# Joining two sequences' causal attentions into one call of eight head groups

## The reference

```
q = (x @ Wq).reshape(b, t, 16, 8) * 8 ** (-0.25)
k = (x @ Wk).reshape(b, t, 16, 8) * 8 ** (-0.25)
v = (x @ Wv).reshape(b, t, 16, 8)
dot = einsum('bqhd,bkhd->bhqk', q, k)
dot = where(causal, dot, -inf)
out = einsum('bhqk,bkhd->bqhd', softmax(dot), v).reshape(b, t, 128)
return out @ Wo
```

## Time and profile before

| | us |
|---|---|
| median of three runs (4137.76 to 4142.01) | 4139.68 |
| the profiled execution | 4147.65 |
| its span, first to last instruction | 4145.7 |
| PE busy in the span | 3816.1 (92%) |
| DVE, ACT, POOL busy | 2304.2, 1747.5, 813.5 |
| mean granted clock of PE | 0.98 |

### The profile page before, as it was taken

One profiled execution on the slowest core, in us unless ns is written; L12 is line 12 of the kernel. 1 busy time (PEld: TensorE's weight loads), 2 busy tenths in 40 slices (PEclk: granted clock), 3 DMA queues, 4 the chain that ended last, 5 costly groups with the idle time before them and its releaser, 6 DMA issues.

```text
span 4145.7 us, 77057 instructions
## 1 busy us (share of the span) xinstructions
PE 3816.1 (92%) x30311; PEld 2466.6 (59%) x30431; DVE 2304.2 (56%) x7434; ACT 1747.5 (42%) x3560; POOL 813.5 (20%) x1373
## 2 busy tenths in 40 slices
PE   7999999988899999998899989999889998999988
PEld 3555567665455556766545546676654555666665
DVE  4545444677454545467654554546765454454776
ACT  3324333466332433346633242335663334233566
POOL 3102013321110202332011020233302102023330
PEclk9999999999999999999999999999999999999999
DMA  2000000000000000000000000000000000000000
GB/s 81 1 1 1 1 1 1 2 2 1 12 1 1 1 1 1 1 2 2 5 8 1 1 1 1 1 1 2 2 6 7 1 1 1 1 1 1 2 2 6
DMA packets 19694, 17.06 MB, mean 4 GB/s; under 512 B 2604, under 2 KB 18941, under 8 KB 19325
## 3 DMA queue, kind: packets, MB, share of 16 engines
q1 hardware_dynamic: 19325, 11.99, 1.0%
HBM read 9.89 MB, written 2.10 MB: 3 GB/s over the span
## 4 chain that ended last, share of the span: by engine, by line
PE 70%; DVE 11%; ACT 8%; POOL 7%; issue 4%; DVEq 0%; POOLq 0%; SPq 0%
PE banks L1033 8%; PE banks L1047 8%; PE banks L1043 8%; PE banks L926 6%; PE banks L958 5%; POOL work L507 4%; PE banks L970 3%; PE banks L911 3%; PE banks L1142 3%; PE banks L1277 2%; ACT work L783 2%; PE banks L831 2%; ACT work L777 2%; PE banks L1114 2%; PE banks L1087 2%
## 5 line engine op out<-in xcount | busy, mean ns | idle before, releaser
L1454 DVE CUSTOM_DVE_ANT_0 work<-banks,mask_row 128x512 f32<-128x512 f32 (+3 forms) x1024 | 444.2, 487 | 248.3 <-PE banks L926 246.3
L669 ACT ACTIVATE work<-banks 128x384 f32<-128x384 f32 (+1 forms) x768 | 357.6, 532 | 373.9 <-PE banks L958 372.2
L687 ACT ACTIVATE work<-banks 128x512 f32<-128x512 f32 (+1 forms) x384 | 227.7, 596 | 650.7 <-PE banks L1043 641.8
L926 PE MATMUL banks<-work 32*128 32x512 f32 (+3 forms) x2048 | 421.5, 460 | 13.0 <-ACT work L662 13.0
L958 PE MATMUL banks<-work 32*128 32x512 f32 (+3 forms) x2048 | 425.8, 464 | 4.3 <-DVE work L1463 4.3
L474 POOL TENSOR_SCALAR_AFFINE_SELECT work<-work 128x128 f32<-128x128 f32 (+1 forms) x768 | 250.1, 332 | 878.8 <-ACT work L669 860.5
L1531 DVE TENSOR_TENSOR work<-work,banks 128x512 f32<-128x512 f32 (+1 forms) x384 | 261.1, 686 | 280.2 <-PE banks L1047 280.2
L464 POOL TENSOR_TENSOR rstd<-rstd,half 128x4 f32<-128x4 f32 x64 | 64.6, 1009 | 1755.2 <-DVE rstd L1388 1755.2
L1033 PEld LDWEIGHTS banks<-wd,work 128*128 128x128 f32 (+1 forms) x3072 | 359.3, 191 | 49.1 <-issue 49.1
L1033 PE MATMUL banks<-wd,work 128*128 128x128 f32 (+1 forms) x3072 | 361.1, 274 | 0.0
L926 PEld LDWEIGHTS banks<-work 32*128 32x128 f32 x2048 | 232.4, 183 | 167.1 <-DVE work L1454 93.6
(11 more groups left out here) (312 smaller groups left out, 6723.0 us busy)
## 6 DMA issues: line engine op xcount, KB each, us to landing
wg<-in_L_ffn_Wg_dram SPq DMA_DIRECT2D x1, 1376.0 KB
wu<-in_L_ffn_Wu_dram SPq DMA_DIRECT2D x1, 1376.0 KB
x_a<-in_L_attn_a_x_dram SPq DMA_DIRECT2D x4, 256.0 KB, 2.8
x_b<-in_L_attn_a_x_dram SPq DMA_DIRECT2D x4, 256.0 KB, 2.9
wd<-in_L_ffn_Wd_dram SPq DMA_DIRECT2D x2, 512.0 KB
out_dram<-x_a SPq DMA_DIRECT2D x4, 256.0 KB, 2.3
out_dram<-x_b SPq DMA_DIRECT2D x4, 256.0 KB, 2.5
wk_l<-in_L_attn_a_Wk_dram SPq DMA_DIRECT2D x1, 512.0 KB, 6.2
```

The lines of the kernel that those rows point to most:

```text
L669: eng.activation(prob4[:, G % 2, hh, C_AT[j]:C_AT[j] + C_N[j]], bank(column_bank(c))[:, 0:C_N[j]], ACT.Exp).then_inc(s_exp, 1)
L926: m = eng.matmul(bank(k % 3)[:, col:col + N], q4[own, G, P * t:P * t + P], k4[own, G, 0:N], start=True, stop=True)
L1454: m = eng.tensor_tensor_reduce(out=summed[:, k % 2, col:col + N], in0=bank(k % 3)[:, col:col + N], in1=mask_row[:, T - N:T], scale=1.0, sc ...
```

## The change

The attentions of a and b of one layer become one call `attn(p)` with eight groups: g = 0 to 3 are a's, g = 4 to 7 b's. Row and column jobs run through 96 steps with the same distance of 16 between them. What b's call did ahead of its jobs, and what a's did behind them, is put behind single row jobs by a table, `BEHIND`: the norm of b behind row job 27, its eight projections behind 39, 42, 51, 54, 63, 65, 77 and 80, its values behind 67, the transposes of a's output behind 75 and its projection behind 79. These entries go round the same three banks as the row jobs (`PLACES`, `row_bank`), and each waits for the entry three places before it. ACT copies an entry's bank behind exponential k - 18. DVE makes the statistics of b's norm behind row maximum 20 and its rows behind 24; POOL makes the power behind select 2. The tail of a and the head of b fall away.

```diff
+GROUPS = 2 * NG
+JOBS = ROWS4 * GROUPS
 LEAD = 16
-WIDE = JOBS4 - LEAD + 1
-HOOK = JOBS4 - 6
+WIDE = JOBS - LEAD + 1
+HOOK = JOBS - 6
+
+
+BEHIND = {27: ("norm", 0), 39: ("project", 8), 42: ("project", 9), 51: ("project", 10), 54: ("project", 11),
+          63: ("project", 12), 65: ("project", 13), 67: ("values", 0), 75: ("out_columns", 0),
+          77: ("project", 14), 79: ("out", 0), 80: ("project", 15)}
+PLACES = [entry for k in range(JOBS) for entry in [("row", k)] + ([BEHIND[k]] if k in BEHIND else [])]
+PLACE = {entry: at for at, entry in enumerate(PLACES)}
...
+        def row_bank(entry):
+            return PLACE[entry] % 3
...
+        def pool_attn(eng, p):
+            for c in range(JOBS):
+                g, hh, j = c // ROWS4, column_head(c), c % ROWS4 // G4
+                eng.wait_ge(s_exp, JOBS * p + c + 1)
+                v = prob4[:, g % 2, hh, C_COL[j]:C_COL[j] + P]
                 if j == 2:
                     v = bass.AP(v.tensor, v.offset, [list(v.ap[0]), [C_COL[3] - C_COL[2], 2], [1, P]])
                 eng.affine_select(out=v, in_=v, compare_op=ALU.is_ge, fill=0.0, base=0,
                                   pattern=[[0, 2], [1, P]] if j == 2 else [[1, P]],
                                   channel_multiplier=-1).then_inc(s_keep, 1)
+                if c == 2:
+                    pool_norm(eng, attn_call(2 * p + 1))
                 if c == WIDE + 1:
-                    pool_norm(eng, attn_call(n) + 1)
+                    pool_norm(eng, moe_call(2 * p))
...
+        def act_attn(eng, p, scale):
+            def stack(i, bk):
+                eng.wait_ge(p_qk, 2 * GROUPS * p + i + 1)
+                G = i // 2 % NG
+                if i % 2 == 0:
+                    m = eng.activation(q4[:, G, :], bank(bk), ACT.Copy, scale=scale)
+                else:
+                    m = eng.activation(k4[:, G, :], bank(bk), ACT.Identity, bias=k_one[:, 0:1])
+                m.then_inc(p_st, 1)
+
+            def out_columns(n, bk):
+                eng.wait_ge(a_oT, n + 1)
+                eng.activation(xnTs[n % 2][:, :], bank(bk), ACT.Copy).then_inc(a_oTs, 1)
+
...
+                what, i = BEHIND.get(c + LEAD + 2, (None, 0))
+                if what == "norm":
+                    act_norm(eng, attn_call(2 * p + 1), row_bank((what, i)))
+                if what == "project":
+                    stack(i, row_bank((what, i)))
+                if what == "out_columns":
+                    out_columns(2 * p, row_bank((what, i)))
                 if c == HOOK + 2:
-                    act_norm(eng, attn_call(n) + 1, 0)
-            group_columns(eng, n, NG - 1, 6 + (NG - 1) % 2)
-            eng.wait_ge(a_oT, n + 1)
-            eng.activation(xnTs[n % 2][:, :], bank(0), ACT.Copy).then_inc(a_oTs, 1)
+                    act_norm(eng, moe_call(2 * p), 0)
...
-        def pe_attn(eng, n, w):
-            xnT = xnTs[n % 2]
+        def pe_attn(eng, p, w):
+            def wait_place(entry):
+
+                if PLACE[entry] < 3:
+                    return
+                what, i = PLACES[PLACE[entry] - 3]
+                if what == "row":
+                    eng.wait_ge(s_max, JOBS * p + i + 1)
+                elif what == "project":
+                    eng.wait_ge(p_st, 2 * GROUPS * p + i + 1)
+                elif what == "norm":
+                    eng.wait_ge(xnT_ok, attn_call(2 * p + 1) + 1)
+                elif what == "values":
+                    eng.wait_ge(a_v, 2 * p + 2)
+                elif what == "out_columns":
+                    eng.wait_ge(a_oTs, 2 * p + 1)
+                elif what == "out":
+                    eng.wait_ge(x_done, 2 * attn_call(2 * p) + 2)
 
             def project(i):
-                if i >= 4:
-                    eng.wait_ge(p_st, 2 * NG * n + i - 3)
-                elif i >= 2 and attn_call(n) > 0:
-                    eng.wait_ge(x_done, 2 * attn_call(n))
+                if i >= 2 * NG:
+                    bk = row_bank(("project", i))
+                    wait_place(("project", i))
+                else:
+                    bk = pad_bank(i)
+                    if i >= 4:
+                        eng.wait_ge(p_st, 2 * GROUPS * p + i - 3)
+                    elif i >= 2 and attn_call(2 * p) > 0:
+                        eng.wait_ge(x_done, 2 * attn_call(2 * p))
+                who, G = i // (2 * NG), i // 2 % NG
...
+            def project_values(who, bk):
+                xnT = xnTs[who]
+                for t in range(NT):
+                    m = eng.matmul(bank(bk)[:, P * t:P * t + P], xnT[:, P * t:P * t + P], w[:, 0, :],
+                                   start=True, stop=True)
+                m.then_inc(p_v, 1)
...
-                if k >= 3:
-                    eng.wait_ge(s_max, JOBS4 * n + k - 2)
+                wait_place(("row", k))
...
+            def out_columns():
+
+                bk = row_bank(("out_columns", 0))
+                wait_place(("out_columns", 0))
+                eng.wait_ge(a_o, GROUPS * p + NG)
+                for t in range(NT):
+                    m = eng.transpose(bank(bk)[:, P * t:P * t + P], xns[0][:, t, :], ident[:, :])
+                m.then_inc(a_oT, 1)
+
+            def out_rows_of_a():
+                bk = row_bank(("out", 0))
+                wait_place(("out", 0))
+                eng.wait_ge(a_oTs, 2 * p + 1)
+                for t in range(NT):
+                    m = eng.matmul(bank(bk)[:, P * t:P * t + P], xnTs[0][:, P * t:P * t + P], w[:, 1, :],
+                                   start=True, stop=True)
+                    if t % 2 == 1:
+                        m.then_inc(a_y, 1)
+
+            def behind(k):
+                what, i = BEHIND[k]
+                if what == "norm":
+                    wait_place((what, i))
+                    pe_norm(eng, attn_call(2 * p + 1), row_bank((what, i)))
+                elif what == "project":
+                    if i == 2 * NG:
+                        eng.wait_ge(xnT_ok, attn_call(2 * p + 1) + 1)
+                    project(i)
+                elif what == "values":
+                    wait_place((what, i))
+                    project_values(1, row_bank((what, i)))
+                elif what == "out_columns":
+                    out_columns()
+                else:
+                    out_rows_of_a()
+
+            eng.wait_ge(xnT_ok, attn_call(2 * p) + 1)
...
+                if k in BEHIND:
+                    behind(k)
...
+                    if k == 20:
+                        norm_stats(attn_call(2 * p + 1), loaded_x)
+                    if k == 24:
+                        norm_rows(attn_call(2 * p + 1))
+                    if k in BEHIND and BEHIND[k][0] == "values":
+                        eng.wait_ge(p_v, 2 * p + 2)
+                        copy_values(row_bank(BEHIND[k]))
+                    if k in BEHIND and BEHIND[k][0] == "out":
+                        eng.wait_ge(a_y, 2 * (2 * p + 1))
+                        eng.tensor_tensor(xs[0][:, :, :], xs[0][:, :, :],
+                                          bank(row_bank(BEHIND[k])).rearrange("p (t d) -> p t d", t=NT),
+                                          ALU.add).then_inc(x_done, 2)
+                    for g in range(GROUPS - 2):
+                        if k == ROWS4 * (g + 1) + LEAD + 8:
+                            heads_out(g // NG, GROUPS * p + g, 6 + g % 2, rden4)
...
-                for n in range(2):
-                    pe_attn(eng, n, w_a)
+                pe_attn(eng, 0, w_a)
                 for n in range(2):
                     pe_moe(eng, n)
-                for n in range(2, 4):
-                    pe_attn(eng, n, w_b)
+                pe_attn(eng, 1, w_b)
```

## The result

The changed kernel takes 4181.21 us (median of five runs, 4165.82 to 4191.41) against 4139.68 before. The ratio is 1.0096, with a 95% interval of 1.0068 to 1.0123: some 40 us slower. The forecast was 4148 with a range of 4100 to 4172, so the time lies outside it. The direction that I held likeliest (slower, 0.42) is right, the size isn't: 8.6 us of loss were forecast and nearly five times as much came.

What follows compares the result with a forecast made beforehand. TensorE, busy 92% of the span, was taken to bound the kernel. Joining removes 18.57 us per pair, insertions and waits add 19.64: 1.07 longer, 8.6 over eight pairs, so 4148 us, range 4100 to 4172.

Steps and rivals of the forecast that it cites:

- The budget: Seam between a's and b's calls: joining shortens first to last mark from 100.44 to 81.87 us, 18.57 per pair.
- The walk of the waits: Groups with inserted entries: TensorE's time plus waiting on ScalarE and GpSimd adds 19.64 us per pair.
- Norm: b's norm at the first weighing: 1.58 us late for GpSimd, 0.67 for transposes, 0.55 more; 2.80 us.
- Two projections: Groups with entries 39, 42 and 51, 54: copies hold back exponentials, 3.12 us each, 6.24 for both.
- Projections and values: Group with entries 63, 65, 67: 4.65 us longer, of which 3.02 is TensorE's own time.
- The fourth group: Entries 75, 77, 79, 80 (out columns, projection, output, projection): 5.95 us longer, 3.69 of it TensorE's.
- the clock behind the new wait: Behind the late first weighing: a granted-clock fall was given no cost in the 4148 sum.
- rival 4: Clock falls inside the call, or tiling changes cost more: 12 to 20 us in all, 4160 to 4172; chance 0.20.
- the three waits I named for it: In the first pair's seam: TensorE waits of 1.06, 0.68 and 0.82 us, named beside 6.8 us at half clock.
- Rivals 1 and 2: Waits behind insertions hidden (11.3 to 12.5 us per pair, chance 0.13) or half hidden (12.5 to 17.5, chance 0.17).
- rival 2: Waits behind insertions half hidden: insertions cost 12.5 to 17.5 us per pair, time 4091 to 4131; chance 0.17.
- The drains: Tiling changes around inserted entries: 24 more per pair at 0.085 us extra, 2.0 us per pair, left out of the sum.

Runs made afterwards that it cites:

- both edits: Changed kernel with GpSimd's power behind select 7 instead of 2 and ScalarE's copies behind exponential k - 16 instead of k - 18; 4101.91 us, ratio 0.9897.

## Why the prediction was wrong, point by point

**The budget was right.** A group without entries is 12.21 us and the last one 9.90, as said. The head takes 23.53 where the clock is full, and the distance behind it is 12.11 in the one pair where it was full there, 23.6 and 12.1 as said. Nothing in the rows speaks against the 18.57 us per pair that the joining removes. But its 0.8 us for the half clock in a seam was read against the shortest seam, 33.65 us, which has a spell of 3.4 us itself; against 32.56, a seam without one, it is 1.9. So 15 of the 149 us that the joining removes (8 x 18.57) were clock, and the 37 behind the first marks are more than twice that.

**The walk of the waits was nearly right.** Norm: 2.80 forecast, (23.53 - 22.01) + (12.11 - 10.87) = 2.76 measured. Two projections: 3.12, measured 3.19. Projections and values: 4.65, measured 4.96. The fourth group: 5.95, measured 6.45. Sum, with the two projections twice, 20.6 instead of 19.64: the two groups with three and four entries were undersized by 0.3 and 0.5 us. A pair becomes 2.0 us longer instead of 1.07, 16 us instead of 8.6. In part the sums are luck. The walk split the two projections into 1.94 us of TensorE's time and 1.18 of waiting; with the copies moved the first is 1.79, and 1.41 went. In the two fuller groups it had 3.02 and 3.69 us of TensorE's time, where 3.8 and 4.7 are left with the copies moved, and 1.63 and 2.26 of waiting, where 1.15 and 1.71 went. These errors cancelled for the most part. Both mechanisms behind it were shown by taking them away: the copy ahead of the exponentials (1.41 us for two projections), and the power ahead of select 3 (1.52 us at the first mark).

**The step that failed is the clock behind the new wait.** The sum behind 4148 has it at nothing, and rival 4, which names it, was given 0.20 and priced at 1 to 3 us per fall, 12 to 20 over all pairs. (1 to 3 us in eight pairs are 8 to 24; its 4172 is the end of the 24.) The fall came in seven pairs of eight and cost 36.9 us, 6.8 to 8.4 us in four of them. With 16 us of the walk this makes 53 us; the heads gave back 1.7, the tails 1.5 and the rest of the program 5.7, and the profiled executions lie 44 us apart. Two arguments misled me. I sized a fall by the one spell I had rows for, 6.8 us in the first seam, as if its length were a property of the chip; here it lasted 20.5. The trace of the kernel before had longer ones behind b's tails, six of 10.2 us and more, the longest this (columns as in the earlier trace rows):

```profile
1192.40:1206.10 13.70, 12.29 (x33) 7.71 (x35) 5.35 (x17) 3.76 (x6) 0.00 (x0) 0.50 0.00 0
```

And I took as evidence against it that the clock stayed at 1.00 for 11 us behind the tail's wait of 1.61 us. That wait has a part in a later fall: cut to 0.77, it left spells of 3.4 us behind the tails of the joined kernel where six were 10.2, and three of six long ones in the kernel before. Nor was the seam's fall the work of the three waits I named for it: it begins at 96.7, and of the three only the one of 1.06 us (94.36) lies ahead of it; 0.68 (97.26) stands at its start and 0.82 (105.00) behind its end.

**Rivals 1 and 2** (the waits hidden) fall for the kernel as it was changed, but their time is that of the kernel with the copies moved: 4105 lies in rival 2's 4091 to 4131.

**The drains** that the Trainium skill's TensorEngine Tiling (Array Packing), section Key Properties, speaks of would have cost 0.085 us more per change, by the estimate in the prediction. With the copies out of the way two projections take 1.79 us in all, 0.89 each, which is the distance from one projection to the next in the earlier trace rows, 0.88, and leaves nothing for the changes. No cost of changing shows in these distances.

**The range** had to reach further up because its worst case was priced at 1 to 3 us per pair; four pairs of eight lay far beyond that. The two fastest of the five executions, 4165.82 and 4169.84, lie inside the range.

**What stays open** is what sets the length of a spell. 17 us and more came only where the wait at the first weighing and held-back exponentials came together (the changed kernel, and the one with one exponential held back); with the wait alone it was 3.4 us, with the held-back exponentials alone there was none, and in the kernel before with the wait added 3.4 or 6.9. Why the same call has a long spell in one pair and a short one in the next these runs don't tell apart.

## What to carry to other kernels

When work is inserted into a full engine's stream, price the queues of its partners too: put a copy behind the last partner instruction whose input is already issued, not in front of it (here one index, worth 76 us by the medians, of which 45 are distances), and put a helper engine's side job behind the instruction for which the full engine waits. Price a new wait of TensorE by two terms, its length and the clock behind it, and for the second take at least the longest spell in the traces, not the nearest one, with TensorE's full work in it (0.42 us lost for each us at 0.50 here). Even that would have been short, with 13.7 us before and 20.5 after. Insertions are cheapest where the engine waits anyway: a projection in front of a wait of 0.72 us got 0.4 to 0.8 us for nothing.

## What the runs showed of the hardware

A single wait of 1.45 us let the granted clock fall from 1.00 to 0.50 in a stretch that was otherwise busy (7.80 of 9.40 us, of which the wait is nearly all the rest). TensorE then was busy in all of the following 20.5 us and the clock stayed at 0.50. With the wait filled by matmuls on constants the clock stayed at 1.00 in all eight pairs. The Trainium skill's TensorE: Matmul & The Clock Gate, section A second HAM failure mode: psum-queue depth-cycling, tells of a kernel whose frequent short idle moments between groups of matmuls make the clock swing between its two levels. The rows here agree that short idle moments are enough, and show more: a single wait of 1.45 us at one place. And time won at one place was in part lost to the clock at another: with both edits the heads were 1.5 us shorter in the mean than with the copies moved alone, and six of the eight tails 1.2 to 1.8 us longer.
